# Layernorm statistics all on VectorE, and the normalised tiles written by GpSimd

## The reference, cut to what matters

```python
xn = layernorm(x)                       # over 2048 features, eps 1e-5
# branch A: W_in (2048 -> 2*4096), split x, z; conv_w (4096 -> 4096) on x
#           y = x * D * silu(z); W_out (4096 -> 2048)
# branch B: relu(xn W1 + b1), relu(. W2 + b2), . W3 + b3
out = x + branchA(xn) + branchB(xn)
```

## Time and profile before

| what | us |
|---|---|
| median of three runs (2044.89 to 2046.14) | 2045.78 |
| the profiled execution's own time | 2044.05 |
| its span, slowest core | 2042.5 |
| span of the fastest core | 2034.4 |
| PE busy | 2002.1 |
| DVE, ACT, POOL busy | 125.3, 189.1, 29.4 |

### The profile page before, as it was taken

One profiled execution on the slowest core, in us unless ns is written; L12 is line 12 of the kernel. 1 busy time (PEld: TensorE's weight loads), 2 busy tenths in 40 slices (PEclk: granted clock), 3 DMA queues, 4 the chain that ended last, 5 costly groups with the idle time before them and its releaser, 6 DMA issues.

```text
span 2042.5 us, 21560 instructions; the slowest of 8 cores (2034.4 to 2042.5 us)
## 1 busy us (share of the span) xinstructions
PE 2002.1 (98%) x9292; PEld 908.9 (44%) x9292; DVE 125.3 (6%) x201; ACT 189.1 (9%) x296; POOL 29.4 (1%) x53
## 2 busy tenths in 40 slices
PE   5999999999999999999999999999999999999998
PEld 2444444444444444444444444444444444444443
DVE  1000011113000000000300000111100000000000
ACT  4121100000002100010011211000000121001000
POOL 0000000000000000000000000000000000000000
PEclk9999999999999999999999999999999999999999
DMA  6444466587465434464664444444434644444352
GB/s 208 149 152 154 145 210 218 182 246 202 137 200 150 144 144 155 154 186 154 199 193 153 148 143 162 147 150 159 145 104 164 199 152 144 158 152 147 132 201 77
DMA packets 69614, 332.94 MB, mean 163 GB/s; under 512 B 15617, under 2 KB 15746, under 8 KB 42898
## 3 DMA queue, kind: packets, MB, share of 16 engines
q1 hardware_dynamic: 64626, 306.36, 45.6%
q0 software_dynamic: 4896, 25.20, 4.3%
HBM read 321.05 MB, written 8.39 MB: 161 GB/s over the span
## 4 chain that ended last, share of the span: by engine, by line
PE 95%; DMA 4%; ACT 1%; issue 0%; SPq 0%; DVE 0%; POOL 0%; ACTq 0%; DVEq 0%; POOLq 0%
PE pmm L397 76%; PE pmm L448 19%; DMA sWr<-W6S 2%; DMA sWr<-W3S 1%; DMA sIDB<-IDB 0%; ACT sRB L229 0%; ACT sXN L567 0%; PE ptrf L553 0%; PE pmm L340 0%; SPq L147 0%; ACT L229 0%; ACT sST L263 0%; DVE sX L514 0%; SPq L152 0%; POOL OUT L521 0%
## 5 line engine op out<-in xcount | busy, mean ns | idle before, releaser
L397 PE MATMUL pmm<-sRA,sWr 128*128 128x512 bf16 x4096 | 885.0, 379 | 0.0
L397 PE MATMUL pmm<-sXN,sWr 128*128 128x512 bf16 x3072 | 664.7, 379 | 0.4 <-ACT sXN L567 0.4
L397 PEld LDWEIGHTS pmm<-sRA,sWr 128*128 128x128 bf16 x4096 | 400.7, 98 | 483.6 <-issue 0.8
L397 PEld LDWEIGHTS pmm<-sXN,sWr 128*128 128x128 bf16 x3072 | 300.7, 98 | 363.6 <-issue 2.0
L448 PE MATMUL pmm<-sWr,sRB 128*128 128x512 bf16 x2048 | 444.0, 379 | 7.1 <-DMA sWr<-W6S 4.5
L448 PEld LDWEIGHTS pmm<-sWr,sRB 128*128 128x128 bf16 x2048 | 199.8, 98 | 250.5 <-issue 11.4
L500 ACT ACTIVATE sRA<-pmm,sCN 128x512 bf16<-128x512 f32 x64 | 44.0, 687 | 610.6 <-PE pmm L397 610.6
L488 DVE SCALAR_TENSOR_TENSOR sRB<-pmm,sCN,sRB 128x512 bf16<-128x512 f32 x64 | 48.0, 751 | 845.2 <-PE pmm L397 845.2
L514 DVE TENSOR_TENSOR sX<-pmm,sX 128x512 f32<-128x512 f32 x64 | 44.2, 691 | 881.9 <-PE pmm L448 881.9
L500 ACT ACTIVATE sRB<-pmm,sCN 128x512 bf16<-128x512 f32 x64 | 44.0, 687 | 400.9 <-PE pmm L397 400.9
L473 ACT ACTIVATE sRA<-pmm 128x512 bf16<-128x512 f32 x64 | 38.2, 597 | 297.3 <-PE pmm L397 297.3
(11 more groups left out here) (31 smaller groups left out, 39.3 us busy)
## 6 DMA issues: line engine op xcount, KB each, us to landing
sWr<-W1S SPq DMA_DIRECT2D x128, 512.0 KB, 3.9
sWr<-W2S SPq DMA_DIRECT2D x64, 1024.0 KB, 5.7
sWr<-W5S SPq DMA_DIRECT2D x64, 1024.0 KB, 5.4
sWr<-W3S SPq DMA_DIRECT2D x32, 1024.0 KB, 6.5
sWr<-W4S SPq DMA_DIRECT2D x64, 512.0 KB, 4.2
sWr<-W6S SPq DMA_DIRECT2D x32, 1024.0 KB, 8.0
sX<-X POOLq DMA_DIRECT2D x8, 1024.0 KB, 10.5
sX<-BB POOLq DMA_DIRECT2D x8, 1024.0 KB, 17.5
```

The lines of the kernel that those rows point to most:

```text
L397: ins = e.matmul(p_mm[b][:], sWr[:, base * 2048 + k * 128:base * 2048 + (k + 1) * 128], rhs_tensor[:, k * TSP:(k + 1) * TSP], start=(k == ...
```

## The change

Tiles 2 and 3 get their statistics from DVE as tiles 0 and 1 do. The passes on ACT and the small operations behind them go. `emit_xn_tm` moves from DVE to GpSimd for all four tiles and counts a semaphore of its own, for which PE's transposes wait.

```diff
+    sem_gp = Ctr("gp")
...
-        def act_accum(j, which, first):
...
-        def act_meansq(j, v_ab):
...
-        def dve_var(j, v_d):
...
         def emit_xn_tm(j, v_rstd):
             sb = j * 32
-            wait("vector", sem_act, v_rstd)
-            op("vector", lambda e, j=j, sb=sb:
+            wait("gpsimd", sem_act, v_rstd)
+            op("gpsimd", lambda e, j=j, sb=sb:
                e.tensor_scalar(sRA[:, j * HID:(j + 1) * HID],
...
-               .then_inc(sem_dve.h, 1))
-            return sem_dve.inc()
+               .then_inc(sem_gp.h, 1))
+            return (sem_gp, sem_gp.inc())
 
         def emit_trf(j, v_xntm):
-            wait("tensor", sem_dve, v_xntm)
+            wait_guards("tensor", [v_xntm])
...
         plan_ln_stats_j(0, 0, v_aggr0)
         plan_ln_stats_j(0, 1, v_aggr0)
-        vA2 = act_accum(2, 0, True)
         rstd0[0] = plan_rstd_j(0, 0, v_aggr0[0])
         vx = {0: emit_xn_tm(0, rstd0[0])}
-        vA3 = act_accum(3, 0, True)
+        plan_ln_stats_j(0, 2, v_aggr0)
         rstd0[1] = plan_rstd_j(0, 1, v_aggr0[1])
         vx[1] = emit_xn_tm(1, rstd0[1])
-        vB2 = act_accum(2, 1, False)
-        vD2 = act_meansq(2, vB2)
-        vE2 = dve_var(2, vD2)
-        rstd0[2] = plan_rstd_j(0, 2, vE2)
+        plan_ln_stats_j(0, 3, v_aggr0)
+        rstd0[2] = plan_rstd_j(0, 2, v_aggr0[2])
         vx[2] = emit_xn_tm(2, rstd0[2])
-        vB3 = act_accum(3, 1, False)
-        vD3 = act_meansq(3, vB3)
-        vE3 = dve_var(3, vD3)
-        rstd0[3] = plan_rstd_j(0, 3, vE3)
+        rstd0[3] = plan_rstd_j(0, 3, v_aggr0[3])
         vx[3] = emit_xn_tm(3, rstd0[3])
```

More of the change, by code:

```diff
@@ L108, in build_program @@
                  for t in range(2)]
-        for c in sem_ws + sem_xt + sem_c + sem_xb + sem_tk + [sem_pe, sem_act, sem_dve, sem_out, sem_warm]:
+        for c in sem_ws + sem_xt + sem_c + sem_xb + sem_tk + [sem_pe, sem_act, sem_dve, sem_out, sem_warm, sem_gp]:
             c.h = ctx.enter_context(nc.semaphore(c.name))
```

## The result

The changed kernel takes 2063.48 us in the median of ten runs, the kernel before 2045.96 beside it: 17.5 us more. The ratio of the two is 1.0102, with a 95% interval of 1.006 to 1.0144. The forecast was 2047.0 with a range from 2044.0 to 2057.0.

The account below looks back on a forecast made before the run. The prediction took the start of the first weight matmul, 32.96 us, as what the change can move. A start 0.9 us late plus 0.3 us for PE's pace gave 1.2 us: from 2045.78 to about 2047.0, range 2044.0 to 2057.0.

Parts of the forecast that it names:

- What bounds: Head before the 2048 matmuls: the change acts only through the first product's start, 32.96 us, each microsecond moving the end by about one.
- Statistics: DVE takes all four tiles' statistics, 2.76 us a tile, last aggregate ending at 23.52 us; this alone could start the product 0.9 us early.
- the table load: ACT's 1.28 us load moves behind tile 0's statistics, 15.34 to 16.62 us; its price is on the path only through GpSimd's start.
- The law for the product's start: First weight matmul starts at 19.9 + 4T or at 32.08 us, whichever is later; forecast 33.9 us, 0.9 us late.
- T: Time of one 128x2048 normalising `tensor_scalar` on GpSimd: estimated 3.5 us, bounded between 0.80 and 6.0 us.
- The rival of slow GpSimd: Normalisation on GpSimd takes 6.0 us a tile, product starts at 43.9 us, time 2057.0 us; decides from T = 4.3; chance 0.28.
- Blocking: Rival in the head: DVE's statistics passes and GpSimd's `tensor_scalar` can't run side by side; time 2052.9 us; chance 0.07.
- PE's pace: Start of the first product: the fast matmul pace may begin later, costing 0.3 us; as a rival 3.4 us, median 2050.1, chance 0.02.

Follow-up runs that it names:

- the early copies: Kernel before, nothing on GpSimd; VectorE takes the transposes' copies of tiles 0 and 1 and half of those of tiles 2 and 3: 2042.34 us against 2045.97, ratio 0.998.

## Why the prediction was wrong

**What bounds.** Right: the change acts only through the start of the first product. Start and time move the same way in every run, though not by the same amount: 15.85 and 17.5 us in the change, -4.1 and -3.6 with the early copies, 2.8 and 4.6 from tile 1 to tile 3 on GpSimd. The rest lies in the pace of the product's beginning and in waits for weights further on.

**Statistics.** Right. The last aggregate ends at 23.27 (forecast 23.52), the table load stands behind tile 0's at 15.27 (15.34), GpSimd starts at 17.36 (17.33). Moved alone, they leave the time at a ratio of 1.0001, and together with the other half they cost what the table load puts on GpSimd's start, 0.87 us, the only way in which the prediction had the load on the path.

**The law for the product's start.** Right: 19.9 + 4T with the measured T of 7.23 gives 48.8 us, and 48.81 was measured.

**T.** This is the step that failed. I took 3.5 us, one slow pass of 3.0 "since a single input read once should not cost two passes" and 0.5 for starting and finishing, and bounded it from above by 6.0. It is 7.23 us, twice the value and above the bound. The 0.5 was near (some 0.3 is fixed); the pass is what was mis-sized, 6.9 us and not 3.0. The upper end was no bound at all: it priced GpSimd's passes at VectorE's slowest row, and nothing in the trace says that GpSimd is as quick as that. The measured makeup is another one: 3.4 ns a column for the two-operation form whatever the type, 1.8 us of it for the second operation, and a copy at 1.89. The prediction said that no row showed arithmetic on POOL; with the end of the range open above, the slow case should have had the larger chance. It had 0.28, and a T above 6.0 only 0.1. The error of 3.73 us in T enters four times, 14.9 us, which is the miss in the product's start (33.9 and 48.8).

**The rival of slow GpSimd** was the right one, with its decision point at 4.3 us; only its price, 10.9 us at T = 6.0, was too low. The rule cited for it, in the opening of the Trainium skill's GPSIMD Engine Reference, that VectorE is roughly twice as fast, points the right way, but the trace has a factor of 7.23/0.80 = 9 for this instruction. The same page's table in section 4.1, by which one-input work runs at about line rate, fits the copy (1.89 us, as ACT's pass of 1.90) and not `tensor_scalar`. Its two-input figure of section 3.1, 4497 ns in fp32, stands beside 4.05 us for a bf16 product here.

**Blocking.** It doesn't decide anything: `bn_stats` keeps its 668 ns beside GpSimd, and GpSimd's instruction is 7.23 us with VectorE busy or idle. That is as the Trainium skill's page SBUF — State Buffer (section "Who interferes with whom") has it for an instruction with one SBUF input outside the 2-port modes. VectorE's own `tensor_scalar` and its two-input step are held up, by up to 1.9 and 3.9 us.

**PE's pace.** The first product took 442.81 us on core 1 where it took 442.19: 0.6 us lost against 0.3 forecast. In the mean over the eight cores it is 0.5 us (441.8 to 443.0 before and 442.5 to 443.1 after, up to the first matmul of W_out), and on core 3 it took less than before, so the size is loosely known. The granted clock reads 1.00 in both, at the slow first matmuls too. Of the 17.0 us by which the eight spans grew, 16.0 are the start and 0.5 the first product. The last 0.5 us are only partly shown: on core 1 there is a wait of 0.8 us for weights, and it was not tried whether that wait follows from the later start or comes and goes.

## What to carry to other kernels

Before work is moved to an engine that has done none of its kind in the trace, measure that one instruction there, in its exact form: a probe on the idle engine in the kernel before would have given 7.24 us at once. A work item moved off an engine that wasn't the bound costs nothing only while the new engine stays ahead of the chain, here by the law above with up to 3.05 us a tile; covered time is a matter of place in the order, as tiles 1 and 3 show. And the gain lay in the row that the chain named, the copies behind the last Exp: giving them to an engine that stood idle took 0.2 to 0.26% off.

## What the runs showed of the hardware

- GpSimd's `tensor_scalar` of 128 x 2048 takes 7.24 us with two operations, 5.44 with one; 3.78 and 2.07 for 1024 and 512 columns; the same in bf16 and fp32. A copy takes 1.89, a two-input product 4.05.
- VectorE's one-column `scalar_tensor_tensor` with two SBUF inputs took 4.00 to 4.01 us on all eight cores when it came 0.65 us after the start of a `tensor_scalar` of GpSimd (7.23 us), and was through 4.66 us after that start; its twin, which came 4.66 us after such a start, took 0.16. VectorE's `tensor_scalar` of 1024 columns took 0.53 to 1.11 us beside GpSimd's of the same size, and that of 2048 columns, which came 5.1 us after GpSimd's start, took 2.66 instead of 0.75 and ended 0.5 us after GpSimd. GpSimd was not slowed. VectorE thus waits for a part of GpSimd's instruction, not always for its end; which part stays open.
- The first matmuls of the product stand 0.43 us apart for some 2 us, the pace of 1.2 GHz for 512 columns, while the granted clock reads 1.00 on all cores of both kernels.
